# First tanh and second exponential of a second attention moved forward, and a feed-forward way out moved into the attention's turning bank

## The reference

```python
x = x + _layernorm(_L0_attn_ref(_layernorm(x), ...))   # a: causal attention with rope
x = x + _layernorm(_L0_ffn_ref(_layernorm(x), ...))    # b: gated feed-forward, below
x = x + _layernorm(_L1_attn_ref(_layernorm(x), ...))   # c: differential attention, below
x = x + _layernorm(_L1_ffn_ref(_layernorm(x), ...))    # d: eight weighted experts
```

```python
# b, with 512 hidden columns
h = silu(x @ w1.T * s1) * (x @ w2.T * s2)
h = gelu(h @ h1.T * sh1)
h = gelu(h @ h2.T * sh2)
return h @ w3.T * s3
# c, 8 heads, per head two query/key pairs of 8 columns and 16 value columns
L1 = einsum(l2norm(q1), l2norm(k1)) * cos_scale
L2 = einsum(l2norm(q2), l2norm(k2)) * cos_scale
G  = tanh(delta_gain * (L1 - L2))
A1 = softmax(L1 + G); A2 = softmax(L2 - G)
y  = (A1 - lambda_full * A2) @ v       # then a norm per head, and the output product
```

## Time and profile before

| | |
|---|---|
| median of 3 runs | 696.75 us (696.32 to 696.86) |
| profiled execution | 696.34 us |
| its span | 694.4 us |
| PE busy | 626.7 us (90%) |
| DVE busy | 523.6 us (75%) |
| ACT busy | 488.3 us (70%) |
| POOL busy | 209.8 us (30%) |
| stage a, 0 to 74.3 us | ACT 44.51, PE 67.04, DVE 54.23 |
| stage b, 74.3 to 234 us | PE 159.20, ACT 54.74, DVE 60.17 |
| front of stage c, 234 to 262 us | PE 25.23, ACT 26.38, DVE 24.24 |
| stage c, 262 to 592 us | ACT 323.60, DVE 315.10, PE 282.49 |
| stage d, 592 to 694.4 us | PE 92.72, DVE 69.85, ACT 39.09 |

### The profile page before, as it was taken

The page is one execution under the profiler, slowest core; times in us unless marked ns, Lnnn a source line. Parts: engine busy times, 40 slices in busy tenths (PEclk is TensorE's granted clock), DMA queues, the critical chain, the costliest instruction groups (busy, mean ns, idle before and its releaser), DMA issues.

```text
span 694.4 us, 9384 instructions
## 1 busy us (share of the span) xinstructions
PE 626.7 (90%) x3289; PEld 272.3 (39%) x3324; DVE 523.6 (75%) x966; ACT 488.3 (70%) x504; POOL 209.8 (30%) x296
## 2 busy tenths in 40 slices
PE   8899999999999999889888888788888887899996
PEld 4677445464464423222322212122222111366555
DVE  6877603328155399999899999999999999676775
ACT  4656424234333599999999999999999999444432
POOL 4423330112102041491147200804701575021012
PEclk9999999999999999999999999999999999999999
DMA  5440200002204401234022510121012203300171
GB/s 170 112 165 1 93 1 0 2 0 67 70 1 137 113 18 41 58 106 137 9 58 88 163 40 19 58 58 57 2 56 58 57 1 124 121 1 1 52 223 31
DMA packets 33230, 44.60 MB, mean 64 GB/s; under 512 B 5408, under 2 KB 20000, under 8 KB 32800
## 3 DMA queue, kind: packets, MB, share of 16 engines
q1 hardware_dynamic: 33184, 44.01, 21.5%
HBM read 31.60 MB, written 10.55 MB: 61 GB/s over the span
## 4 chain that ended last, share of the span: by engine, by line
PE 38%; ACT 26%; DVE 21%; issue 11%; DMA 1%; POOL 1%; SPq 0%; DVEq 0%; ACTq 0%
ACT w_hh L1146 20%; PE ps L780 8%; PE ps L790 8%; DVE hid L1491 5%; DVE hid L1486 5%; PE ps L815 4%; PE ps L761 4%; PE ps L693 3%; PE ps L674 2%; ACT probs L1117 2%; PE ps L824 2%; DVE st L1248 2%; PE ps L747 2%; PE ps L587 1%; DMA x_res<-in_x 1%
## 5 line engine op out<-in xcount | busy, mean ns | idle before, releaser
L1146 ACT ACTIVATE w_hh<-hid 128x2048 f32<-128x2048 f32 x128 | 251.3, 1964 | 5.8 <-DVE hid L1491 5.4
L693 PE MATMUL ps<-w_hh,v_h 128*32 128x512 f32 x1024 | 136.4, 604 | 34.6 <-ACT w_hh L1146 33.1
L1486 DVE TENSOR_TENSOR hid<-ps,probs 128x1024 f32<-128x1024 f32 x86 | 104.7, 1218 | 20.7 <-ACT probs L1117 16.1
L1491 DVE SCALAR_TENSOR_TENSOR hid<-ps,probs 128x1024 f32<-128x1024 f32 x86 | 104.9, 1220 | 4.9 <-PE ps L674 3.6
L674 PE MATMUL ps<-q_s,k_s 64*128 64x512 bf16 x256 | 98.7, 386 | 10.2 <-DVE hid L1486 9.7
L674 PE MATMUL ps<-q_w,k_w 64*128 64x512 bf16 x256 | 98.7, 386 | 0.0
L1117 ACT ACTIVATE probs<-ps 128x1024 f32<-128x1024 f32 x86 | 92.2, 1072 | 1.1 <-PE ps L674 1.1
L674 PE MATMUL ps<-q_g,k_s 128*128 128x512 bf16 x221 | 69.6, 384 | 5.9 <-issue 5.1
L674 PEld LDWEIGHTS ps<-q_w,k_w 64*128 64x128 bf16 x256 | 23.7, 92 | 105.9 <-issue 57.0
L790 PE MATMUL ps<-hid,w_hh 128*128 128x512 f32 x128 | 56.3, 592 | 0.0
L780 PE MATMUL ps<-hid,w_hh 128*128 128x512 f32 x128 | 55.8, 593 | 0.0
(11 more groups left out here) (352 smaller groups left out, 1016.1 us busy)
## 6 DMA issues: line engine op xcount, KB each, us to landing
qk_rows<-part SPq DMA_DIRECT2D x48, 128.0 KB, 2.4
w_hh<-w_rows SPq DMA_DIRECT2D x4, 1024.0 KB, 9.0
qk_rows<-part_g SPq DMA_DIRECT2D x24, 128.0 KB, 2.4
q_g<-qk_rows SPq DMA_DIRECT2D x32, 96.0 KB, 2.2
k_s<-qk_rows SPq DMA_DIRECT2D x32, 96.0 KB, 2.3
q_s<-qk_rows SPq DMA_DIRECT2D x32, 96.0 KB, 2.4
k_w<-qk_rows SPq DMA_DIRECT2D x32, 96.0 KB, 2.5
q_w<-qk_rows SPq DMA_DIRECT2D x32, 96.0 KB, 2.4
```

Of the source, the lines that this page charges most:

```text
L693: last = mm(ps[VW * g4:VW * g4 + VW, 6, :], v_h[:, u, mt, :], ee[:, mt % 2, g4 * CHUNK:(g4 + 1) * CHUNK], start=(mt == 0), stop=(mt == BT ...
L1146: A(ee[:, mt % 2, :], zz[:, mt % 2, :], ACT.Exp).then_inc(S["e"], 1)
L1486: v.tensor_tensor(zz[:, mt % 2, 0:SEQ], banks[:, 2 * CHUNK:4 * CHUNK], gg[s % 3], ALU.add).then_inc(S["z1"], 1)
L1491: v.scalar_tensor_tensor(zz[:, mt % 2, SEQ:2 * SEQ], banks[:, 4 * CHUNK:6 * CHUNK], -1.0, gg[s % 3], ALU.mult, ALU.subtract).then_inc(S["z ...
```

## The change

- **ACT**: tanh 0 moves from behind the last Gelu to behind the h2 Gelu 1 of the last chunk, with a small Exp ahead of it, and `c_evac(2)` moves behind Gelu 2. Between the exponentials 0 and 1 and behind them the order becomes exponential 0, tanh 2, exponential 1, tanh 3, tanh 4, exponential 2; from step 3 on it is the old one. Exponential 0 waits for `z1` too.
- **PE**: difference 0 and the turn of chunk 2 move in front of the h2 group 3, with their waits. `c_second(0)` comes ahead of `c_first(0)`. The way out's tile 0 and 1 are in the prologue, tile 2 at the end of step 2 and tile 3 at the end of step 4, all into the turning bank. The steps 0 and 1 of the loop are written out in front of it in another order.
- **DVE**: `z_second(0)` comes ahead of `z_first(0)`; `b_evac(3)` moves from step 1 to step 5, `b_stats(3)` from step 2 to step 6.
- **The table**: the uses `raw` 0 and 1 move from the steps 2 and 5 to the steps 6 and 7. `raw` 0 waits for the way out to be read.

```diff
--- before.py
+++ after.py
@@ -67,7 +67,7 @@
 NH = BATCH * HEADS
 
 
-SPECIAL = {(0, 2): ("raw", 0), (0, 5): ("raw", 1), (1, 1): ("v", 0), (1, 3): ("sums", 0), (2, 1): ("scale", 0),
+SPECIAL = {(0, 6): ("raw", 0), (0, 7): ("raw", 1), (1, 1): ("v", 0), (1, 3): ("sums", 0), (2, 1): ("scale", 0),
            (2, 3): ("scale", 1), (3, 1): ("late turn", 0), (3, 3): ("raw", 2), (3, 5): ("raw", 3), (3, 7): ("v", 1),
            (4, 5): ("sums", 1), (5, 3): ("scale", 2), (5, 5): ("scale", 3),
            (9, 7): ("y", 0), (10, 1): ("wo", 0), (10, 3): ("y", 1), (10, 5): ("wo", 1), (11, 5): ("x", 0),
@@ -627,6 +627,7 @@
                 elif kind == "raw":
                     if i == 0:
                         pe.wait_ge(S["xt_c"], CHUNKS - 1)
+                        pe.wait_ge(S["yo_b"], CHUNKS)
                     last = c_raw(i % 2, turn)
                 elif kind == "v":
                     last = c_v()
@@ -749,6 +750,7 @@
                 return last
 
             pe.wait_ge(ld["bw"], 48)
+            late_c = CHUNKS - 1
             for c in range(CHUNKS):
                 pe.wait_ge(S["xt_b"], c + 1)
                 for m in range(KT_):
@@ -790,6 +792,11 @@
                         last = mm(ps[:, o, :], w_h2[:, k, o * P:(o + 1) * P], hid[:, 1, k, :],
                                   start=(k == 0), stop=(k == KT_ - 1))
                     last.then_inc(S["m2_b"], 1)
+                    if (c, o) == (late_c, 2):
+                        pe.wait_ge(S["g2_b"], KT_ * late_c + 2)
+                        pe.wait_ge(load[0], 16 * OWN)
+                        c_diff(0, 0, 0)
+                        c_prep_turn(late_c - 1)
                     if 1 <= c < CHUNKS - 1:
                         if o == 0:
                             c_prep_turn(c - 1)
@@ -853,28 +860,33 @@
                 pe.wait_ge(S["wo_read"], 2)
                 router(c, ps[:, 6, :], (c - 2) * CT * EXPERTS).then_inc(S["rt_d"], 1)
 
-            pe.wait_ge(load[0], 16 * OWN)
-            late_c = CHUNKS - 1
-            pe.wait_ge(S["g2_b"], KT_ * late_c + 2)
-            c_diff(0, 0, 0)
             pe.wait_ge(cross[0], 16 * CROSSED)
+            pe.wait_ge(S["yo_b"], late_c)
+            pe.wait_ge(S["qh_c"], 2)
+            c_second(0, 0, 0)
+            c_diff(1, 0, 1)
             pe.wait_ge(S["g2_b"], KT_ * CHUNKS)
             c_first(0, 0, 0)
-            pe.wait_ge(S["yo_b"], late_c)
-            c_second(0, 0, 0)
-            c_prep_turn(late_c - 1)
-            pe.wait_ge(S["qh_c"], 2)
-            b_out_tile(late_c, 0, ps[:, 6, :])
-            c_diff(1, 0, 1)
-            b_out_tile(late_c, 1, ps[:, 6, :])
+            pe.wait_ge(S["xt_c"], late_c)
+            b_out_tile(late_c, 0, turn)
+            c_first(1, 0, 1)
+            c_second(1, 0, 1)
             c_diff(2, 0, 2)
-            c_first(1, 0, 1)
-            b_out_tile(late_c, 2, ps[:, 6, :])
-            c_second(1, 0, 1)
-            b_out_tile(late_c, 3, ps[:, 6, :]).then_inc(S["y_b"], 1)
+            c_first(2, 0, 2)
+            pe.wait_ge(S["vh"], 1)
+            c_values(0, 0, 0)
+            c_second(2, 0, 2)
+            c_diff(3, 0, 3)
+            b_out_tile(late_c, 1, turn)
+            c_first(3, 0, 3)
+            c_diff(4, 0, 4)
+            c_values(1, 0, 1)
+            c_second(3, 0, 3)
             for n in range(NH):
                 for mt in range(BT):
                     s = n * BT + mt
+                    if s < 2:
+                        continue
                     later = s + 2 < NH * BT
                     n2, mt2 = divmod(s + 2, BT)
                     if s + 3 < NH * BT:
@@ -898,11 +910,13 @@
                     if mt == 0:
                         pe.wait_ge(S["vh"], n + 1)
                         pe.wait_ge(S["accout"], n)
-                        if n == 0:
-                            pe.wait_ge(S["yo_b"], CHUNKS)
                     c_values(s, n % 2, mt)
                     if later:
                         c_second(s + 2, n2 % 2, mt2)
+                    if s == 2:
+                        b_out_tile(late_c, 2, turn)
+                    if s == 4:
+                        b_out_tile(late_c, 3, turn).then_inc(S["y_b"], 1)
 
 
             downs = 0
@@ -1072,6 +1086,12 @@
                 act.wait_ge(S["gr1_c"], c + 1)
                 A(part_g[:, 1, :], g_q[:], ACT.Copy).then_inc(S["gmid_c"], 1)
 
+            def tanh_step(s, u, mt):
+                act.wait_ge(S["dd"], s + 1)
+                if s >= 3:
+                    act.wait_ge(S["z2"], s - 2)
+                A(gg[s % 3], banks[:, 0:2 * CHUNK], ACT.Tanh).then_inc(S["g"], 1)
+
             act.wait_ge(ld["bw"], 48)
             me.mark(A(tiny[:, 57:58], s_b[:, 0:1], ACT.Silu))
             for c in range(CHUNKS):
@@ -1099,6 +1119,11 @@
                     if c:
                         act.wait_ge(S["y_b"], c)
                     A(hid[:, 2, o, :], ps[:, o, :], ACT.Gelu, scale=s_b[:, 12 + o:13 + o]).then_inc(S["g2_b"], 1)
+                    if (c, o) == (CHUNKS - 1, 1):
+                        me.mark(A(tiny[:, 58:59], tiny[:, 0:1], ACT.Exp))
+                        tanh_step(0, 0, 0)
+                    if (c, o) == (CHUNKS - 1, 2):
+                        c_evac(CHUNKS - 2)
                     if 1 <= c < CHUNKS - 1:
                         if o == 0:
                             c_evac(c - 1)
@@ -1110,12 +1135,6 @@
                     A(tiny[:, 8:17], tiny[:, 8:17], ACT.Tanh).then_inc(S["fact_c"], 1)
 
 
-            def tanh_step(s, u, mt):
-                act.wait_ge(S["dd"], s + 1)
-                if s >= 3:
-                    act.wait_ge(S["z2"], s - 2)
-                A(gg[s % 3], banks[:, 0:2 * CHUNK], ACT.Tanh).then_inc(S["g"], 1)
-
             def d_gate(b):
 
                 if b == 0:
@@ -1131,19 +1150,24 @@
                 A(rt[:, 4], rt[:, 2], ACT.Exp, scale=-1.0 / 0.3).then_inc(S["ex_d"], 1)
 
             me.mark(A(tiny[:, 56:57], tiny[:, 0:1], ACT.Exp))
-            tanh_step(0, 0, 0)
-            c_evac(CHUNKS - 2)
             tanh_step(1, 0, 1)
             for n in range(NH):
                 for mt in range(BT):
                     s = n * BT + mt
-                    if s + 2 < NH * BT:
+                    if 2 < s < NH * BT - 2:
                         n2, mt2 = divmod(s + 2, BT)
                         tanh_step(s + 2, n2 % 2, mt2)
                     act.wait_ge(S["z2"], s + 1)
+                    if s == 0:
+                        act.wait_ge(S["z1"], 1)
                     if s == NH * BT - 1:
                         act.wait_ge(S["av"], s - 1)
                     A(ee[:, mt % 2, :], zz[:, mt % 2, :], ACT.Exp).then_inc(S["e"], 1)
+                    if s == 0:
+                        tanh_step(2, 0, 2)
+                    if s == 1:
+                        tanh_step(3, 0, 3)
+                        tanh_step(4, 0, 4)
                     if (n, mt) == (13, 1):
                         d_gate(0)
                     if (n, mt) == (13, 5):
@@ -1649,18 +1673,22 @@
                 u = n % 2
                 for mt in range(BT):
                     at = (n, mt)
+                    if at == (0, 0):
+                        dve.wait_ge(S["g"], 1)
+                        z_second(0, 0)
                     z_first(n * BT + mt, mt)
                     if mt == 1 and n:
                         acc_out(n - 1)
-                    z_second(n * BT + mt, mt)
-                    if at == (0, 1):
-                        b_evac(CHUNKS - 1, ps[:, 6, :])
+                    if at != (0, 0):
+                        z_second(n * BT + mt, mt)
+                    if at == (0, 5):
+                        b_evac(CHUNKS - 1, turn)
 
                     use = turning(*divmod(n * BT + mt - 1, BT)) if n * BT + mt else None
                     if use:
                         turn_out(use)
 
-                    if at == (0, 2):
+                    if at == (0, 6):
                         b_stats(CHUNKS - 1)
                     if use and use[0] == "sums":
                         dve.wait_ge(S["turn_read"], turns_done(use))
```

## The result

The changed kernel takes **698.68 us** (median, 698.45 to 699.01) against 696.59 us for the kernel before on the same chip: a ratio of 1.0027 with a 95% interval of 1.0016 to 1.0038. It is 2.09 us slower. Its profiled execution took 698.64 us, with a span of 696.8, which is 2.4 over the span of before.

The account below looks back on a forecast made before the run. ScalarE sets the second attention's 2.70 us steps, VectorE close behind. Front -1.28, steps 2 to 6 +2.03 and steps 6 to 10 +1.64 sum to +2.39 us: 699.0 us forecast, range 697.3 to 700.3, slower at 0.73.

Parts of the forecast that it names:

- The sum: Whole kernel: -1.28 + 2.03 + 1.64 = +2.39 us, giving 698.7 to 699.1, stated as 699.0.
- The front: Up to exponential 2: early tanh 0 gains 1.28 us, with both added table loads hidden in ScalarE's idle time.
- Steps 2 to 6: Exponential 2 to 6, with moved way-out tiles: 13.38 us against 11.35 before, 2.03 more.
- The late tanh 6: ScalarE behind way-out tile 2: tanh 6, due 248.90, starts at 249.45, so 0.55 us is lost.
- The stall: VectorE idles some 2.4 us for tile 3 ahead of the step 6 sums; exponential 6 comes 2.03 late.
- Steps 6 to 10: VectorE without lead pays for statistics, two raw copies and the accumulator copy: 12.46 us against 10.82, 1.64 more.
- A: Rival, faster: VectorE's lead covers the late tile, so only the front counts, 695.4 us; chance 0.10.
- B: Rival, within 0.2%: stall present but pile-up smaller, or front gives 2.47; +0.75 (697.5) or +1.2; chance 0.17.
- D: Rival, worse: head 0's rows land late or the load back to gelu costs more; +2.7 to +3.4 us; chance 0.13.
- The Trainium skill's drain: At each ScalarE table switch: about 1.38 us added to the 1.28 load, 2.66 in all; given 0.03 within D.
- The batching rule: ScalarE at the front: batch activations by table set, which the added round trip into the tanh set undoes.
- The reserve of VectorE: VectorE's two sums per step take 2.35 of 3.50 us: reserve 1.15, often 0.9 when the second waits for TensorE.

Follow-up runs that it names:

- run with the late tanh: Changed kernel with difference 0, the turn of chunk 2, tanh 0 and chunk 2's copy back behind all h2 groups or the last gelu: 700.65 us, ratio 1.0058.
- copy in step 6: Changed kernel with VectorE's way-out copy moved from step 5 to 6 and its statistics from step 6 to 7: 697.18 us, ratio 1.0009.
- tile 3 in front: Changed kernel with tile 3 of the way out ahead of the first product and values of step 4, not behind them: 696.54 us, ratio 1.0001.
- spread kernel: Changed kernel with tiles 2 and 3 ahead of the values, way-out copy in step 6, statistics in step 11, squares and roots first: 695.42 us, ratio 0.9990.
- front alone: Kernel before with only early difference 0, turn of chunk 2 and tanh 0, and difference 1 ahead of first product 0: 695.62 us, ratio 0.9987.

## Why the prediction was right

- **The sum.** Forecast +2.39 on the profiled execution, measured, counted from gelu 1: -1.38 + 1.93 + 1.65 - 0.04 = +2.16. Between the medians it is 2.09. 699.0 was forecast, 698.68 measured.
- **The front.** -1.28 forecast, -1.38 measured. The path is the forecast one: tanh 0 ahead of gelu 2 (the prediction counts the h2 groups from 1, so its group 4 is the one of gelu 3) and, counted from gelu 1, exponentials 0, 1 and 2 each within 0.15 us of their forecasts. That the added table loads cost nothing at gelu 3 is shown by the trace, and the run with one more load shows how little cover is left. The run with the late tanh shows that the early tanh carries 1.87 of it. What I had not seen is that the reordering by itself costs 0.49 and that the early tanh doesn't need it.
- **Steps 2 to 6.** +2.03 forecast, +1.93 measured. The late tanh 6 was put at 0.55; it is 0.40, because this tile costs the difference behind it 0.99 (247.82 to 248.81), not 1.09, and the values start 1.96 and not 2.0 behind their exponential. The stall was put at 2.4 us and is 2.52; exponential 6 was to come 2.03 later than due and comes 2.05 later. The copy in step 6 takes 1.64 out of this part and tile 3 in front takes 2.05 out.
- **Steps 6 to 10.** +1.64 forecast, +1.65 measured: exponentials 7, 8, 9 and 10 were forecast at 3.44, 2.86, 3.46 and 2.70 apart and are 3.43, 2.86, 3.46 and 2.72 apart. The statistics' share of it is shown (1.10); that of raw copies and accumulators was not taken out alone.
- **The rivals.** A is excluded by the row with the 2.52 us of idle time and by the runs with the copy in step 6 and with tile 3 first. B and D are excluded by the parts of the table, D also by difference 0, which didn't wait. The Trainium skill's drain behind a table load (ScalarE: Activation LUTs, "What ACT_TABLE_LOAD costs") is shown by no row here: the next activation starts 0.01 to 0.02 behind a load, and a second load 0.02 behind the small activation. The prediction's sum by that rule is wrong: with the 2.66 us of the Trainium skill the load back to gelu would end, by this estimate, at 233.96 (231.30 + 2.66), before its group 4 (234.21) and not after it; late would be gelu 3, behind gelu 2 and the copy. The batching rule of the same page of the Trainium skill ("Table sets: the hidden batching unit") would have spoken against the front, and the front alone is faster here, because both added loads lie ahead of a gelu that waits for TensorE.
- **Where the reasoning was thin.** The reserve of VectorE was counted as 0.9 to 1.15 everywhere. It is a balance of both engines: a tile or a raw product on TensorE uses it too, not only a copy on VectorE. The expectations for the copy in step 6 and for the spread kernel missed by 0.6 and by 0.2 to 0.8, and in their rows VectorE waits for TensorE where a full reserve had been counted; that this is the whole of it isn't shown.

## What to carry to other kernels

In a loop in which each engine works in order, put work that one engine makes and another takes at least a full step apart, and count from what the maker's queue waits for just ahead of it: here a 1 us tile stood behind values that waited for an exponential, and its taker stood ahead of the sums that ScalarE needed. In these runs small extras were free only as long as both engines of a step had a lead, and they belong where an engine waits anyway. When a change bundles several moves, price each by itself: here the first move alone gains 1.0 us and the others give back 3.1.

## What had not been expected of the hardware

A table load doesn't stand beside the activation that needs it: the load for gelu is at 231.56, directly behind tanh 0, and in the kernel before one runs at 205.63 whose gelu starts at 209.24, after 2.32 us of waiting for TensorE. So this load came early without a small activation ahead of it; whether the small Exp of this kernel is needed wasn't tried.

Two more figures are worth keeping. One row isn't the price of a group: a tile of four 128-column f32 products takes 0.95 to 0.99 us from start to start in most rows here, but 1.09 in others (239.02 to 240.11 in the kernel before, the piece of the earlier trace rows), and no run shows why. And gelu 1, up to which the kernels are the same, comes up to 0.53 us earlier or later from one profiled execution to the next, so a difference of a few tenths has to be counted from a point behind it.
